# Self-attention's lower halves in two instructions of 512 columns, one signal each

## The reference

```
x = x + attention(layer_norm(x), layer_norm(x))   # 16 heads of 64, over 1024 keys
x = x + attention(layer_norm(x), context)         # 77 context tokens of 192 columns
x = x + geglu_ff(layer_norm(x))                   # 256 -> 2*1024 -> 256
attention: softmax(q k^T / 8) v per head, then @ wo + bo
```

## Time and profile before

| What | Value |
|---|---|
| Median of 3 runs (lowest, highest) | 2147.9 us (2145.25, 2148.32) |
| The profiled execution: its own time, its span | 2148.0 us, 2146.3 us |
| PE, DVE, ACT, POOL busy, share of the span | 97%, 75%, 69%, 64% |
| Granted TensorE clock, mean | 0.997 |
| Chain that ended last, shares | PE 80%, DVE 8%, ACT 5%, issue 3%, POOL 2% |

### The profile page before, as it was taken

How to read it: one execution, slowest core, us unless ns; L and a number is a source line. 1 busy time by engine, 2 the same in 40 slices (tenths; PEclk the granted TensorE clock), 3 DMA queues, 4 the chain that set the end, 5 groups by cost and what they waited for, 6 DMA issues and landing times.

```text
span 2146.3 us, 58872 instructions
## 1 busy us (share of the span) xinstructions
PE 2078.8 (97%) x25120; PEld 1413.0 (66%) x25120; DVE 1607.8 (75%) x3014; ACT 1473.6 (69%) x1950; POOL 1372.4 (64%) x860
## 2 busy tenths in 40 slices
PE   6999999999999999999999999999999999999999
PEld 2666666775666666678466666667746666667675
DVE  6888887657688888765868888866577888886664
ACT  4888888345488888834548888874455888886442
POOL 6878887453378887744347888774424888775540
PEclk8999999999999999999999999999999999999999
DMA  4322230050332232004032233100403323210120
GB/s 138 78 56 66 67 75 24 11 105 18 81 89 66 56 82 63 19 16 100 25 94 75 66 78 78 46 29 10 96 20 92 85 67 81 64 39 21 31 55 20
DMA packets 132581, 127.82 MB, mean 60 GB/s; under 512 B 81760, under 2 KB 94048, under 8 KB 132320
## 3 DMA queue, kind: packets, MB, share of 16 engines
q1 hardware_dynamic: 132080, 123.66, 23.0%
q10 hardware_dynamic: 240, 0.39, 0.1%
HBM read 55.72 MB, written 4.19 MB: 28 GB/s over the span
## 4 chain that ended last, share of the span: by engine, by line
PE 80%; DVE 8%; ACT 5%; issue 3%; POOL 2%; DMA 1%; SPq 1%; POOLq 0%; DVEq 0%; ACTq 0%
PE work L1018 9%; PE scores L1042 8%; PE scores L1035 8%; PE scores L927 7%; PE scores L929 7%; PE scores L928 6%; PE work L1064 5%; PE work L1060 5%; PE work L1062 5%; PE work L927 4%; PE work L929 4%; PE work L928 4%; ACT prob L1415 2%; DVE minima L1615 1%; PE work L1072 1%
## 5 line engine op out<-in xcount | busy, mean ns | idle before, releaser
L864 POOL TENSOR_TENSOR prob<-prob 128x1024 f16<-128x1024 f32 x328 | 709.0, 2178 | 295.4 <-ACT prob L1415 279.4
L1615 DVE TENSOR_REDUCE minima<-work 128x1 f32<-128x512 f32 x1024 | 681.6, 683 | 60.8 <-PE work L1018 55.2
L1414 ACT ACTIVATE prob<-scores 128x1024 f32<-128x1024 f32 x512 | 528.3, 1032 | 96.2 <-PE scores L1042 76.3
L1415 ACT ACTIVATE prob<-scores 128x1024 f16<-128x1024 f32 x512 | 524.8, 1025 | 0.0
L1060 PE MATMUL work<-vals,prob 128*128 128x65 f16 x4096 | 428.8, 192 | 9.4 <-POOL prob L864 6.1
L1060 PEld LDWEIGHTS work<-vals,prob 128*128 128x128 f16 x4096 | 383.0, 99 | 73.0 <-issue 20.0
L1064 PE MATMUL work<-vals,prob 128*128 128x65 f16 x4096 | 429.4, 195 | 0.0
L1062 PE MATMUL work<-vals,prob 128*128 128x64 f16 x4096 | 429.2, 193 | 0.0
L1062 PEld LDWEIGHTS work<-vals,prob 128*128 128x128 f16 x4096 | 379.8, 96 | 52.8
L1018 PE MATMUL work<-ka,qa 128*128 128x512 f16 x1024 | 390.1, 384 | 21.8 <-DVE minima L1615 16.1
L1064 PEld LDWEIGHTS work<-vals,prob 128*128 128x128 f16 x4096 | 380.2, 97 | 0.0
(11 more groups left out here) (168 smaller groups left out, 4156.6 us busy)
## 6 DMA issues: line engine op xcount, KB each, us to landing
qa<-staged_q SPq DMA_DIRECT2D x128, 128.0 KB, 2.3
ka<-staged_k SPq DMA_DIRECT2D x126, 128.0 KB, 2.3
raw_even<-in_pairs SPq DMA_DIRECT2D x32, 384.0 KB, 3.3
raw_odd<-in_pairs SPq DMA_DIRECT2D x32, 384.0 KB, 3.4
raw_odd<-in_pieces SPq DMA_DIRECT2D x20, 512.0 KB, 3.3
raw_even<-in_pieces SPq DMA_DIRECT2D x20, 512.0 KB, 3.4
qb<-staged_q SPq DMA_DIRECT2D x64, 128.0 KB, 2.3
kb<-staged_k SPq DMA_DIRECT2D x63, 128.0 KB, 2.3
```

The lines of the kernel that those rows point to most:

```text
L864: pool.tensor_tensor(prob[1][:, slot, :], prob32[:, slot, :], prob[0][:, slot, :], ALU.subtract).then_inc(a.polished, 1)
L1414: act.activation(prob32[:, n % RING, :], source, ACT.Exp)
L1415: act.activation(prob[0][:, n % RING, :], source, ACT.Exp)\
L1615: dve.tensor_reduce(minima[:, t, h:h + 1], out[:, :], AX.X, ALU.max, negate=True)\
```

## The change

A polish and a refine become two subtracts of 512 columns, one for each key tile, each with its own increment. PE's value step waits for the first half's count before the first key tile and for the second half's count before the second key tile. Nothing else is changed: the same columns are subtracted by the same engines in the same order of steps, and cross-attention keeps its subtracts of 1024 columns.

```diff
                     elif step.kind == "polish":
                         slot = pace.slot(step)
                         pool.wait_ge(a.exp_done, pace.tiles(step) + SCORE_RING)
-                        pool.tensor_tensor(prob[1][:, slot, :], prob32[:, slot, :],
-                                           prob[0][:, slot, :], ALU.subtract).then_inc(a.polished, 1)
+                        for i in range(2):
+                            cols = slice(i * BLK, (i + 1) * BLK)
+                            pool.tensor_tensor(prob[1][:, slot, cols], prob32[:, slot, cols],
+                                               prob[0][:, slot, cols], ALU.subtract).then_inc(a.polished, 1)
...
-                        pe.wait_ge(a.polished if pace.polished(step) else a.refined, pace.lows(step))
+                        lows = a.polished if pace.polished(step) else a.refined
+                        pe.wait_ge(lows, 2 * pace.lows(step) - 1)
                         first = s % KEY_STEPS == 0
...
                         for i, k in enumerate([2 * (s % KEY_STEPS) + i for i in range(2)]):
+                            if i:
+                                pe.wait_ge(lows, 2 * pace.lows(step))
                             v = vals[par][:, k, head, :]
...
                     elif step.kind == "refine":
                         slot = pace.slot(step)
                         dve.wait_ge(a.exp_done, pace.tiles(step) + SCORE_RING)
-                        dve.tensor_tensor(prob[1][:, slot, :], prob32[:, slot, :],
-                                          prob[0][:, slot, :], ALU.subtract).then_inc(a.refined, 1)
+                        for i in range(2):
+                            cols = slice(i * BLK, (i + 1) * BLK)
+                            dve.tensor_tensor(prob[1][:, slot, cols], prob32[:, slot, cols],
+                                              prob[0][:, slot, cols], ALU.subtract).then_inc(a.refined, 1)
```

## The result

The changed kernel takes 2240.7 us (median of 4 runs, 2239.5 to 2242.1) against 2148.1 us (4 runs beside it, 2145.3 to 2149.0). The ratio is 1.0434 with a 95% interval of 1.0416 to 1.0452: slower, inside the predicted range of 2170 to 2245, 12 us above the predicted 2229. The profiled span is 2237.7 us against 2146.3.

A forecast was written before the change was run, and what follows sets the result against it. PE, busy 97% of the span, was taken as the bound; three contacts of POOL between refine halves (31, 17 and 33 us, other terms 0) added 81 us to 2148, giving 2229 us, range 2170 to 2245.

The forecast's parts named there:

- What comes between two halves: A waiting POOL instruction goes between a refine's halves on DVE and delays DVE's queue: 81 us over four rounds.
- A: Step 3 of odd units: POOL's split subtract goes between refine halves; max matmul 1.12 us late, 28 times, 31 us.
- B: Step 7 of odd units 3 to 11: POOL's subtract goes between; projection 0.86 us late, 20 times, 17 us.
- C: Step 1 of even units 4 to 10: half a polish goes between; max and value 2.04 us late, 16 times, 33 us.
- POOL's additional instructions: Polishes in halves on POOL: 0.15 us more for each of 328, 49 us of POOL, hidden by slack.
- PE's second wait: One wait more in each of 512 value steps on PE: taken as 0, at most 5 us in all.
- the early signal: PE's four waits of 1.5 us for POOL's lower halves could shrink: gain between 0 and 6.1 us, taken as 0.
- DVE's additional instructions: Refines in halves on DVE: 0.06 us more for each of 184, 11 us of DVE; taken as 0 on PE.
- DVE keeps its turn: Rival, chance 0.10: POOL is not let in between refine halves, only longer instructions cost; 2150 us.
- Short contacts: Rival, chance 0.20: POOL's position moves once PE is late, so contacts cost less; 2189 us, range 2170 to 2205.
- Shorter holds: Rival, chance 0.05: a refine meeting a running polish, as in unit 2, waits for half of it; 2143 us.
- The signs: Expected in the trace: POOL's subtract between refine halves, max waits for DVE some 60 us, POOL's waits for ACT little changed.

The follow-up runs named there:

- e6: Kernel before the change, only the refines of tile 2 in odd units (32 of 184, asked for in step 3) in halves: 2183.7 us, ratio 1.0164.
- e7: Kernel before the change, only refines of tile 0 in odd and tile 7 in even units in halves, no POOL instruction waiting there: 2150.4 us, ratio 1.0012.
- e4: Changed kernel, with POOL's splits waiting for both refine halves in step 3 and 7 of odd and step 1 of even units: 2203.8 us, ratio 1.0263.
- e8: Kernel before the change, only the refines of tile 0 in even units (asked for in step 1) in halves: 2157.1 us, ratio 1.0043.
- e9: Kernel before the change, only the refines of tile 6 in odd units (asked for in step 7) in halves: 2146.7 us, ratio 0.9999.
- e2: Changed kernel with POOL's polishes whole again (increment of two), DVE's refines still in halves: 2282.6 us, ratio 1.0636.
- e1: Changed kernel with DVE's refines whole again (increment of two), POOL's polishes still in halves: 2160.6 us, ratio 1.0062.
- e3: Changed kernel with polishes and refines both whole (increments of two), only PE's second wait kept: 2154.4 us, ratio 1.0029.
- e5: As e4, but in step 1 of even units POOL waits ahead of the split's first instruction: 2183.0 us, ratio 1.0163.
- e11: As e5, but the refine of tile 3 in even units is one instruction with an increment of two: 2176.8 us, ratio 1.0135.
- e10: Kernel before the change, all whole; POOL's polish of tile 2 in units 2 and 12 waits for DVE's refine: 2171.4 us, ratio 1.0107.

## Why the prediction was right, step by step

**What comes between two halves: right, and shown.** e6 and e7 split it: the same edit costs 36 us where a POOL instruction waits and 2.5 us, for nearly twice as many halves, where none does. e4 takes nearly all of the odd units' loss away by holding POOL back, with all the halves in place. And POOL came first wherever it was waiting: in all 82 places of the changed kernel, in 27 of 27 in e6, 20 of 20 in e8 and 27 of 27 in e9; in e7 there was no such place.

**A: the max right, the term too small.** 1.12 us predicted at the max, 1.14 measured. Left out was the next instruction on DVE: the staging of oT behind the reduce. Before, it ended at 250.60, just ahead of the projection that needs its bank at 250.66; this is DVE's row of before:

```profile
249.93 0.68 DVE L1586 TENSOR_TENSOR oT<-work,oT 128x512 f16<-128x512 f32 x1
```

By the prediction's own working its reduce ends at 251.51, so the staging ends 0.60 later at 252.11, and the projection starts at 252.17 in place of 251.57 + 0.21: 0.39 us more, and 0.38 was measured. The prediction also counted one place too many: in the last round unit 13 has no split left and goes from 20.77 to 20.93 us only. So A is 27 x 1.52 = 41 us in place of 31, and these 10 us are most of the 12 us between 2229 and 2240.7. The failure is one of method: A was followed as far as the first matmul that is late, and not to the end of DVE's queue.

**B and C: right in size, in the changed kernel.** B 0.86 predicted, 0.43 + 0.38 = 0.81 measured. C 2.04 predicted (1.18 at the max and 0.86 at the value), 1.42 + 0.62 = 2.04 measured. That C's sums agree to the last digit is luck: its two parts are off by 0.24 us, one each way. But neither is a cost of its own refine: alone they cost 0 (e9) and 0.55 us (e8), because POOL then meets the gap with another, shorter instruction. The terms were right because they were walked with A's delay and with POOL's longer polishes in them. A, B and C alone sum to some 45 us; together with POOL's halves they are 92.6. A's delay makes C dear even without POOL's halves: in e2 even units take 24.45 us at the full clock, in e8, without A, 21.34.

**POOL's additional instructions: taken at zero, wrongly as a statement by itself.** Alone they cost 13 us (e1), some of it the experiment's increments of two. In the change their 2.28 us stands inside B and C, so the sum did not miss them.

**PE's second wait and the early signal: zero, right.** e3's odd units do not move. In unit 14, where the four waits of 1.5 us were the earlier trace rows, the unit goes from 18.54 to 18.45 us: the first key tile starts early and the second waits for the rest. **DVE's additional instructions:** 0.07 us in e7's odd units, within the bounds.

**The rivals.** "DVE keeps its turn" falls by the timeline. "Short contacts" has the sizes that e8 and e9 show, but not those of the change. "Shorter holds" gained PE nothing that a run shows. Unit 2 is 0.6 us shorter in each round, 2.4 us in all, but no shorter hold is there: POOL stands idle when its refine comes, and the two halves take 1.28 us with no POOL instruction ahead of them:

```profile
101.76 1.28 DVE L1633 TENSOR_TENSOR prob<-prob 128x512 f16<-128x512 f32 x2
```
```profile
102.81 5.74 POOL L866 TENSOR_TENSOR prob<-prob 128x512 f16<-128x512 f32 x5 [1.30 <-ACT prob L1420]
```

In e6, where the polishes and this refine are whole, unit 2 gains as well (20.78 in place of 21.75 us, in three of four rounds): A's delay in unit 1 has moved the two apart. Less waiting behind a shorter instruction does show, off PE's path, in POOL's split subtract: 2056 ns behind half a refine in place of 2598 behind a whole one. That is what the Trainium skill's page SBUF — State Buffer (Who interferes with whom) would give, an exclusive lock for the whole of an instruction; here the trace agrees. The prediction found nothing there on who comes next when one engine has two in a row. The Trainium skill's SBUF — State Buffer (Who interferes with whom) does say in general that issue order decides who blocks. The 82 places agree: POOL's instruction was issued before DVE's second half.

**The signs.** All but one came as listed. POOL's waits for ACT, which were to change little, grew from 279.4 us to the 355.7 of the first table; no run shows why. This is the row of before:

```profile
POOL prob L864 <- ACT prob L1415: 279.4, 104, 10.6
```

**What stays open.** e5 and e11 leave even units at 22.37 and 22.08 us. In e1, where POOL's program is as long but POOL neither waits nor meets a gap, they take 21.64 us, the refines' increments of two included. What lies above that in e5 and e11 is POOL's wait and what is left of the collisions, and the two were not separated.

## What to carry to other kernels

Where two engines shut each other out for whole instructions, cutting an instruction in two is an offer to the other engine: look for what is waiting there, and carry its length down the whole queue behind the second part, to every matmul that a reduce, a staging or a gather releases. Price such places together, since each delay decides which instruction the next gap meets. A wait on the off-path engine can win that time back (37 us in e4), but only if what stands behind the wait has slack (e10 lost 24, about half of it by the clock).

## What the runs showed of the hardware that was not expected

An increment of two on a subtract became an instruction of its own, 512 of them in e3, which took 6.5 us longer in all.

A PE that stops can come back slower. In e10, unit 12, PE waited 2 us for a polish, and the granted clock fell behind it. By stretches of 2 us (busy us of PE, PEld, DVE, ACT and POOL with instructions, then the granted clock, the DMAs' share and GB/s):

```profile
320.00:322.00 2.00, 0.25 (x8) 0.26 (x9) 1.10 (x4) 1.49 (x2) 2.00 (x2) 1.00 0.89 210
322.00:324.00 2.00, 2.00 (x27) 1.09 (x24) 0.69 (x1) 0.00 (x0) 2.00 (x2) 0.75 0.85 206
324.00:326.00 2.00, 2.00 (x27) 1.62 (x26) 0.85 (x2) 1.66 (x2) 1.87 (x1) 0.50 0.16 63
```

0.50 is the lower level, 1.2 GHz. The stop and the clock make unit 12 3.0 us longer. In unit 2 an equal stop at 102.9 to 104.9 left the clock at 1.00, and there the unit is 1.3 us longer. In the profiled execution the clock fell in all four units 12, in one unit 2 and in three units 14; such a unit takes some 1.6 us more than the same unit at 1.00 (unit 2: 24.68 against 23.05). Eight of them make some 13 us, an estimate from these lengths. In e2 the mean granted clock is 0.987 against 0.997 before; from 290 to 295 us of it, where a whole polish goes between two halves, PE is busy 2.93 of 5 us and the clock is 0.79 (0.87 in the next 5 us).
